# Preparing the feed-forward weights inside the K/V stage instead of in a stage of their own

## The reference

```python
# per core: x is 4096 x 1024 (fp32)
x = x + layernorm(attention(layernorm(x), Wq, Wk, Wv, Wo) + bo)   # 16 heads of 64, softmax over 4096 keys
def tlin(x, w, s): return einsum('bsi,oi->bso', x, w) * s          # w: [out, in], s: [out]
h = silu(tlin(y, w1, s1)) * tlin(y, w2, s2)                        # y = layernorm(x); w1, w2: 4096 x 1024
h = gelu(tlin(h, h1, sh1)); h = gelu(tlin(h, h2, sh2))             # h1, h2: 4096 x 4096
x = x + layernorm(tlin(h, w3, s3))                                 # w3: 1024 x 4096
```

## Time and profile before

| | us |
|---|---|
| median of the 3 timed runs (11286.14 to 11311.11) | 11296.86 |
| the profiled execution, its own time | 10338.26 |
| span of the profiled execution, slowest core | 10336.7 |
| spans of the 8 cores | 10305.6 to 10336.7 |
| mean granted TensorE clock of the cores | 0.918 to 0.920 |

### The profile page before, as it was taken

How to read it: one execution, slowest core, us unless ns; L and a number is a source line. 1 busy time by engine, 2 the same in 40 slices (tenths; PEclk the granted TensorE clock), 3 DMA queues, 4 the chain that set the end, 5 groups by cost and what they waited for, 6 DMA issues and landing times.

```text
span 10336.7 us, 101169 instructions; the slowest of 8 cores (10305.6 to 10336.7 us)
## 1 busy us (share of the span) xinstructions
PE 8099.2 (78%) x37812; PEld 3463.8 (34%) x38276; DVE 1873.8 (18%) x2266; ACT 2961.2 (29%) x3427; POOL 352.4 (3%) x687
## 2 busy tenths in 40 slices
PE   3443558686686866868698998998989989899898
PEld 2222222121121211212244444453444444444444
DVE  2222432322223222232201101001011020110100
ACT  3442008475474754747100000001010010000000
POOL 0000000000000000000000000000000000000000
PEclk9999778788787877878899999999999999999999
DMA  9996110101101011010344444334444444444333
GB/s 291 312 314 206 49 57 15 53 5 49 37 17 53 5 49 37 17 53 5 134 150 148 143 155 139 147 145 150 153 145 149 149 145 155 146 148 149 137 154 138
DMA packets 178447, 1214.61 MB, mean 118 GB/s; under 512 B 37185, under 2 KB 37185, under 8 KB 125250
## 3 DMA queue, kind: packets, MB, share of 16 engines
q0 software_dynamic: 88128, 830.51, 22.4%
q1 hardware_dynamic: 89858, 377.60, 11.1%
HBM read 1073.82 MB, written 134.22 MB: 117 GB/s over the span
## 4 chain that ended last, share of the span: by engine, by line
PE 44%; DMA 5%; issue 2%; DVE 1%; ACT 1%; DVEq 0%; SPq 0%; POOLq 0%; ACTq 0%
PE PQ L74 40%; PE PW L74 4%; DMA slab<-w2Ts 2%; DMA slab<-w1Ts 2%; DMA slab<-h1Ts 1%; DMA ybt<-y_s 1%; DVE fs L74 0%; ACT HB L74 0%; DVE ob L74 0%; ACT L74 0%; PE ftr L74 0%; ACT fs L74 0%; DVE HB L74 0%; DVE g_sb L74 0%; DMA yb<-y_s 0%
## 5 line engine op out<-in xcount | busy, mean ns | idle before, releaser
L74 PE MATMUL PQ<-HB,slab 128*128 128x512 bf16 x16056 | 3537.5, 380 | 67.1 <-DMA slab<-h1Ts 27.8
L74 ACT ACTIVATE ptring<-SS,cst 128x1024 bf16<-128x1024 f32 x2048 | 2070.5, 1214 | 896.5 <-PE SS L74 896.5
L74 PEld LDWEIGHTS PQ<-HB,slab 128*128 128x128 bf16 x16384 | 1604.6, 98 | 2000.0 <-issue 78.3
L74 ACT ACTIVATE HB<-PQ 128x1024 bf16<-128x1024 f32 x384 | 392.1, 1023 | 3566.8 <-PE PQ L74 3566.6
L74 PE MATMUL OP<-ptring,v_sb 128*66 128x512 bf16 x4096 | 1210.2, 412 | 88.4 <-DVE ocat L74 81.4
L74 PE MATMUL PQ<-g_sb,slab 128*128 128x512 bf16 x4008 | 937.9, 389 | 319.7 <-ACT HB L74 149.1
L74 PE MATMUL SS<-q_sb,k_sb 64*128 64x512 bf16 x4096 | 1070.0, 396 | 16.5 <-ACT ptring L74 9.0
L74 PE MATMUL ptr<-ident,scb 128*128 128x128 bf16 x2816 | 371.2, 302 | 527.6 <-DVE scb L74 409.1
L74 DVE RECIPROCAL rcp<-OP 1x512 bf16<-1x512 f32 x128 | 420.1, 3317 | 1767.2 <-PE OP L74 1767.1
L74 PEld LDWEIGHTS PQ<-g_sb,slab 128*128 128x128 bf16 x4096 | 395.4, 99 | 860.5 <-issue 441.7
L74 PEld LDWEIGHTS OP<-ptring,v_sb 128*66 128x66 bf16 x4096 | 312.5, 113 | 918.9 <-issue 907.5
(11 more groups left out here) (76 smaller groups left out, 2256.7 us busy)
## 6 DMA issues: line engine op xcount, KB each, us to landing
slab<-h1Ts POOLq DMA_DIRECT2D x128, 2048.0 KB, 8.5
slab<-h2Ts POOLq DMA_DIRECT2D x128, 2048.0 KB, 8.4
natf<-h1w SPq DMA_DIRECT2D x32, 2048.0 KB, 27.1
natf<-h2w SPq DMA_DIRECT2D x32, 2048.0 KB, 27.1
slab<-w1Ts POOLq DMA_DIRECT2D x128, 512.0 KB, 3.8
slab<-w2Ts POOLq DMA_DIRECT2D x128, 512.0 KB, 3.6
slab<-w3Ts POOLq DMA_DIRECT2D x32, 2048.0 KB, 8.6
h1Ts<-stage POOLq DMA_DIRECT2D x16, 2048.0 KB, 17.4
```

Of the source, the lines that this page charges most:

```text
L74: ins = getattr(e, meth)(*args, **kw)
```

## The change

The weight stage is removed as a stage. Its work is cut into 352 steps of 128 x 1024 weights (w1 and w2 32 steps each, h1 and h2 128 each, w3 32), and the steps are written into the lists of the K/V stage: two (`PPP`) after each of its 16 weight casts, after each of the 4 normalised tiles, the 8 K accumulations and the 8 V accumulations of a group, which is 176 places; what is left follows at the end.

A step `prep_step` issues three things: the load of quarter k, the scaling of quarter k-1, and the transposes, copies and stores of quarter k-2. All DMAs of it are on POOL's queue. There are two `natq` buffers (512 KB each), three `pscb`, and two `pstg` buffers of 128 KB; each half of a step is copied into its own `pstg` and stored at once. The scratch layout changes: w1, w2, h1 and h2 are kept by 128 output rows, so a slab of the feed-forward stage is loaded by two DMAs of half the size; w3 keeps its layout, and its stores are therefore made of pieces of 128 bf16 values.

```diff
-    wt_s = {nm: nc.dram_tensor(nm + "Ts", [No // 256, 128, (Ni // 128) * 256],
-                               BF16, kind="Internal").ap()
-            for nm, No, Ni in W_SPECS}
+        if nm == "w3":
+            shape = [No // 256, 128, (Ni // 128) * 256]
+        else:
+            shape = [No // 128, 128, Ni]
...
-        with contextlib.ExitStack() as ps:
-            WMAX = max(D, HID)
...
-            p.emit()
...
+                def prep_load(k):
+                    nm, oc, q, occ, first = QL[k]
+                    npar = k % 2
+                    if first:
+                        slot = occ % 4
+                        if scol_slot_bake[slot]:
+                            p.wait("gpsimd", VE, scol_slot_bake[slot])
+                        scol_ld[occ] = p.dma(
+                            "gpsimd", f"d_pscol{slot}", scol[:, slot:slot + 1],
+                            W_SCL[nm][oc * 128:(oc + 1) * 128][:, None],
+                            allow_slow_non_contiguous=True)
...
+                    if pq_bake[npar]:
+                        p.wait("gpsimd", VE, pq_bake[npar])
+                    ldrec[k] = p.dma("gpsimd", f"d_pnat{npar}", natq[npar][:, :],
+                                     W_NAT[nm][oc * 128:(oc + 1) * 128,
+                                               q * 1024:(q + 1) * 1024])
+
+                def prep_bake(k):
...
+                    p.wait("vector", *ldrec[k])
+                    p.wait("vector", *scol_ld[occ])
+                    if pq_trb[par]:
+                        p.wait("vector", TE, pq_trb[par])
+                    bk = p.op("vector", "tensor_scalar_mul", pscb[par][:, :],
+                              natq[npar][:, :], scol[:, slot:slot + 1], inc=True)
+                    pq_bake[npar] = bk
...
+                def prep_compute(k):
+                    nm, oc, q, occ, first = QL[k]
+                    par = k % 3
+                    p.wait("tensor", VE, bakerec[k])
+                    for b in range(2):
+                        tp = b
+                        if pq_stev[tp]:
+                            p.wait("tensor", AE, pq_stev[tp])
+                        for j in range(4):
+                            trb = p.op("tensor", "transpose",
+                                       ptr[tp][:, j * 128:(j + 1) * 128],
...
+                                       ident[:, :], inc=(j == 3))
+                        p.wait("scalar", TE, trb)
+                        if stg_ch_last[b] is not None:
+                            p.wait("scalar", *stg_ch_last[b])
+                        stev = p.op("scalar", "copy", pstg[b][:, 0:512],
+                                    ptr[tp][:, 0:512], inc=True)
+                        pq_stev[tp] = stev
+                        p.wait("gpsimd", AE, stev)
+                        if nm == "w3":
+                            off = (oc % 2) * 128
+                            dst = wt_s["w3"][oc // 2] \
+                                [:, (q * 8 + 4 * b) * 256:(q * 8 + 4 * b + 4) * 256] \
+                                .rearrange("p (j c) -> p j c", c=256) \
+                                [:, :, off:off + 128]
+                            src = pstg[b][:, 0:512].rearrange("p (j c) -> p j c",
+                                                              c=128)
+                        else:
+                            dst = wt_s[nm][oc][:, (2 * q + b) * 512:
+                                               (2 * q + b + 1) * 512]
+                            src = pstg[b][:, 0:512]
+                        stg_ch_last[b] = p.dma("gpsimd", f"d_pstg{b}", dst, src)
+                    pq_trb[par] = trb
...
+                def prep_step(n=1):
+                    for _ in range(n):
+                        k = prep_ptr[0]
+                        if k >= prep_N + 2:
+                            return
+                        if k < prep_N:
+                            prep_load(k)
+                        if 0 <= k - 1 < prep_N:
+                            prep_bake(k - 1)
+                        if 0 <= k - 2 < prep_N:
+                            prep_compute(k - 2)
+                        prep_ptr[0] += 1
+
+                npoints = 16 + NG * 20
+                PPP = -(-prep_N // npoints)
...
                         wcast += 1
-
-                xb_free = [wcast - 1, wcast]
+                        prep_step(PPP)
...
                             ltr_free[tpar] = ev
+                        prep_step(PPP if b == 1 else 0)
...
                                        KP[:, :], inc=True)
+                        prep_step(PPP)
...
                                                  inc=True)
+                            prep_step(PPP)
+                while prep_ptr[0] < prep_N + 2:
+                    prep_step()
...
+                        p.dma("gpsimd", f"d_slab{spar}",
+                              slab[spar][:, 0:nic * 128], wt_s[nm][2 * og])
                         sld = p.dma("gpsimd", f"d_slab{spar}",
-                                    slab[spar][:, 0:nic * 256], wt_s[nm][og])
+                                    slab[spar][:, nic * 128:nic * 256],
+                                    wt_s[nm][2 * og + 1])
...
-                                          slab[spar][:, ic * 256 + oc * 128:
-                                                     ic * 256 + oc * 128 + 128],
+                                          slab[spar][:, oc * nic * 128 + ic * 128:
+                                                     oc * nic * 128 + ic * 128 + 128],
```

More of the change, by code:

```diff
@@ L157, in build_program @@
         cst = top.enter_context(nc.sbuf_tensor("cst", [128, 4], F32))
-        with contextlib.ExitStack() as ps:
-            WMAX = max(D, HID)
[L161 to L257, removed]
-                        stev = p.op("scalar", "copy", dst, src, inc=True)
-                        ptr_free[tpar] = stev
-                    scb_free[par] = trb
-                    if oc % 2 == 1:
-                        p.wait("gpsimd", AE, stev)
-                        stage_free[og % 2] = p.dma(
-                            "gpsimd", f"d_og{og % 2}", wt_s[nm][og],
-                            stage[og % 2][:, 0:nic * 256])
-                    oc_glob += 1
-            p.emit()
@@ new lines, in build_program @@
+                p.op("gpsimd", "memset", cst[:, 2:3], 0.125)
+                consts_done = p.op("gpsimd", "memset", ones_f[:, :], 1.0, inc=True)
+                p.wait("tensor", GP, consts_done)
+                p.wait("scalar", GP, consts_done)
+                p.wait("vector", GP, consts_done)
+                borow = natq[1][0:1, 0:D]
+                bo_ld = p.dma("sync", "d_bo", borow[:, :], bo_h[None, :])
+                bo_ev = 0
+                for half in range(D // 512):
+                    p.wait("tensor", *bo_ld)
+                    if bo_ev:
+                        p.wait("tensor", VE, bo_ev)
+                    bo_mm = p.op("tensor", "matmul", KP[:, :], ones_f[:, :],
+                                 borow[:, half * 512:(half + 1) * 512],
+                                 start=True, stop=True, inc=True)
+                    p.wait("vector", TE, bo_mm)
+                    bo_ev = p.op("vector", "tensor_copy",
+                                 bo_sb[:, half * 512:(half + 1) * 512], KP[:, :],
+                                 inc=True)
@@ new lines, in build_program @@
+                bo_gate = bo_mm
+                QL = []
+                occ = 0
+                for nm, No, Ni in W_SPECS:
+                    for oc in range(No // 128):
+                        for q in range(Ni // 1024):
+                            QL.append((nm, oc, q, occ, q == 0))
+                        occ += 1
+                prep_N = len(QL)
+                pq_bake = [0, 0, 0]
+                pq_trb = [0, 0, 0]
+                pq_stev = [0, 0]
+                scol_slot_bake = [0, 0, 0, 0]
```

49 lines of the change are left out of this document (45 added, 4 removed).

## The result

The changed kernel is slower: the ratio of its time to that of the kernel before is **1.020** (95% interval 1.018 to 1.022), some 205 us on an execution of 10332 to 10347 us. In some executions of either kernel a die is granted a lower clock and the whole takes up to 10% longer; those are left out of the ratio, and the median of 11297 us from which the prediction started consisted of them alone. So its total (11353) and its range (11060 to 11680) lie far above the 10538 to 10566 us measured here, and only the difference says something: 56 us were forecast, about 205 came.

The account below looks back on a forecast made before the run. The weight stage was taken as bound by DMA engines, the K/V stage by its PE and DVE chain. New K/V stage 1503 us, 17 over the two stages, plus slabs 35 and 4: 56 on 11296.86, so 11353 us, range 11060 to 11680.

Parts of the forecast that it names:

- Which loop: K/V stage: each copy waits for the previous step's store of its half; 3.9 us a step, 352 steps, 1373 us.
- The landing of a small store: In the store loop: a 128 KB store issued by POOL lands after 2.5 us, bounds 2.1 and 7.0.
- 0.1 for other transfers: In each step of the store loop: 0.1 us added to the 3.68 us turn for other DMA traffic.
- DVE holding POOL up: In each step: POOL's DMA issues that meet a DVE scaling wait for its end; 0.1 us added.
- Tiles: K/V stage, normalised tiles: the tile's chain cuts the store loop; 40 us added, at most 67.
- w3: w3's 32 steps: stores in 256-byte pieces take longer; 70 us added, between nothing and 144.
- ends: K/V stage: first load and scaling, two trailing steps and last landing; 20 us added.
- Slabs: Feed-forward stage: slabs fetched in two halves land later; 35 us for w1 and w2, 4 for h1 and h2.
- the four cases: Chances for the whole kernel: forecast 0.38, shorter store loop 0.29, bound by bytes 0.07, lock or contention 0.26.
- The store loop is shorter: K/V stage rival: landing 2.1 us and no lock, 3.3 us a step, -224 us, total 11097; chance 0.29.
- DVE's lock, or other transfers in the way: K/V stage rival: delay at each step, 4.6 us a step, +293, slabs +60, total 11650 us; chance 0.26.
- The transfers overlap: K/V stage rival: steps bound by bytes at 302 GB/s, -397 us, total 10900 us; chance 0.07.

Follow-up runs that it names:

- the padded kernel: Changed kernel with 512 unused columns behind each scratch row of w1, w2, h1, h2; K/V stage ended at 1541 to 1555 us, spans 10379 to 10403.
- the last experiment: Changed kernel with three load buffers, one 256 KB store a step, rows of two output blocks, one transfer a slab; fastest 10113 us, kernel before 10341 to 10355.

## Why the prediction came out as it did

**Which loop (right).** Copy waits for store, store for copy: experiments with more store buffers (-250 us) and with more load buffers (nothing) show it, and the turn is made of the terms named, each found again: 0.08, 0.59 and 0.57 us, where 0.06, 0.59 and 0.53 had been taken.

**The landing of a small store (the step that failed for the difference).** The prediction took 2.5 us, by scaling from larger transfers. Without the weights' loads it is 2.2; beside them, in rows 9 KB apart, 2.5; in rows 8 KB apart, as the change lays them out, 3.1 in the median and 3.27 in the mean of the first halves at K and V places. These 0.77 and the 0.06 of the two hand-overs, less the 0.2 that had been added for POOL and other transfers, are the 0.6 us by which a step is too long. The term "0.1 for other transfers" was meant for the loads and was too small, and no term stood for the layout, which was listed as an edit that "changes no matmul" and not looked at from the store's side. At K and V places a step took 4.50 us instead of 3.9: 256 x 0.6 = 154 us. With rows of 9 KB it is 4.02, a tenth of a microsecond from the forecast. That the layout matters is shown, on all cores and at two other distances; that it acts by the distance of the rows, and not by something that goes with it such as where the tensors begin, was not taken apart. Why 8 KB is worse than 9 and 16 is not shown, nor whether it matters without loads (in the run without them, rows were 8 KB apart and stores landed in 2.2).

**DVE holding POOL up (right, small).** POOL's issues of h1's and h2's stores have a mean of 554 ns. Of the 512 on core 1, 42 overlapped a scaling of DVE and took 0.67 us, the others 0.54; that is 0.01 us a store, well under the 0.1 added and far from the rival's 0.75. The Trainium skill's rule on the two engines (SBUF — State Buffer, "Who interferes with whom") costs little here, because few store issues meet a scaling. The load issues meet one more often, 97 of 352, and then take 0.70 us instead of 0.55.

**Tiles (mis-sized).** 64 steps at tile places took 5.76 us, 1.26 more than those at K and V places, so 81 us against the 40 in the sum; in the padded kernel it is 5.39 against 4.02, some 1.4 more. The prediction took three of four tiles at 0.8 over a step for each pair of steps; no run took the tile's chain apart, so how it misses the other 40 us stays open.

**Casts (missed).** 32 steps beside the loads of `Wk` and `Wv` took 4.75 us instead of 3.9, 27 us. Also in the padded kernel they take 4.7, so it is not the layout. SP's 512 KB loads of `Wk` and `Wv` lie beside these steps; no run took them away, but without the weights' own loads a step there took 3.9 us, 0.2 more than at K and V places, so SP's loads alone are not the whole of it.

**w3 (wrong).** 70 us were added for pieces of 256 bytes. Its steps took 4.2 us and its stores landed after 2.7; POOL's issue is longer (0.75 us in the page of groups), but the turn counts from the start of the issue. Nothing is owed here.

**Sum for the stage, core 1.** 1503 forecast, + 154 (landing) + 27 (casts) + 79 (tiles: 64 x 5.76 = 369 instead of 64 x 3.9 + 40 = 290) - 70 (w3) + 5 (ends) = 1698, measured 1693.

**Slabs (small, over-sized).** 35 us were forecast for w1 and w2. PE's waits for them were 147.5 us on core 1 after and 132.9 before, 141 after on core 2 and 145 on core 0 before: some 15 us at most and within what cores differ by (over die 0 the means are 144 after and 137 before). Half a slab lands after 3.0 us where the whole took 3.6: issued 0.54 later, the second half is there after 3.54, no later than the whole was.

**The total (the step that failed for the level).** Between the median of three runs and the profiled execution lay 959 us, and the prediction carried them over into its total as a constant, because the change touches none of it. They are no property of the kernel: other executions of the kernel before took 10332 to 10347 us. The forecast should have been made for the profiled execution, 10338 + 56, with the level of the timed runs as a case of its own; the range, 959 us lower, is 10101 to 10721 and holds the measured level, but by its width: it also holds the middles of three of the four cases.

**Rivals.** "The store loop is shorter" needed a landing of 2.1 us beside the loads; 2.2 was seen only with the weights' loads left out. "DVE's lock, or other transfers in the way" had the right side, and its 4.6 us a step is near the 4.50 measured at K and V places. It is the second half of its name that came true. Its total, +353 us, is as far above the measured difference as the forecast's +56 is below: it also charged 100 us for w3 and 60 for slabs, which did not come. "The transfers overlap" is reached in part, and only with other buffers and another layout: at 0.80 DMA share and 249 GB/s and not at 302, with a stage of 1251 to 1264 us instead of 1050. The Trainium skill (Perfetto Trace Analysis, "Optimization Strategy") says that interleaving regimes with different contended engines may improve performance; the last experiment agrees (-2.2%), the change as made does not (+2.0%). Between them lie 1.25 us a step.

## What to carry over

When work is moved to lie beside other work, find its smallest loop and the transfer in it, and count buffers: here one buffer for each half put every store's latency into 352 steps, and one more was worth 250 us. A transfer's latency in that loop must be priced beside the traffic that will be there, with the address pattern that it will have; a new layout of a scratch tensor is an edit to its writer as much as to its reader. And where a wait appears twice in a profile (copies for stores, scalings for loads), only relaxing each by itself tells which is slack.

## What the runs showed of the hardware

- A 128 KB store in 128 pieces of 1 KB, beside 512 KB loads, landed after 3.1 us (h1, core 1) with rows 8 KB apart, 2.7 with 16 KB and 2.5 with 9 KB; the loads beside it after 5.0, 4.9 and 4.5. For w1, with rows 2, 4 and 3 KB apart, there was no such order (3.1 and 3.3, 3.3 and 3.7, 3.3, where two runs were made).
- The same store landed after 2.2 us with the weights' loads left out, and after 5.0 with up to four stores and two loads in flight.
- Issued by ACT it took 0.33 us to issue instead of 0.54 and landed after 3.8 us instead of 3.1.
- Stores in pieces of 256 bytes took POOL 0.75 us to issue instead of 0.55, and landed no later than those of 1 KB: after 2.7 us, in rows 16 KB apart, where pieces of 1 KB took 2.6 to 2.8.
- The mean granted clock over the whole K/V stage was 0.68 at 4.75 us a step, 0.70 at 4.34 and 0.77 at 3.50. From 841.40 to 845.10 us, with a clock of 0.50 (the lower of its two levels, 1.2 GHz), eight V matmuls took 3.62 us instead of the 1.89 of eight K matmuls at 1.00 in the earlier trace rows. ACT's next copy, at 845.98, did not wait for them but for the store of `h1Ts` of 840.38, so here the lower clock did not set the time.
